# Query projection of two head groups in one matmul of 128 columns

## What is computed

```
x = x + attention0(layernorm(x), ctx, tau, delta)
x = x + ffn0(layernorm(x))
x = x + attention1(layernorm(x), ctx, tau, delta)
x = x + moe1(layernorm(x))

attention: q = split(xn @ Wq.T + bq); k, v = split(ctx @ Wk.T + bk), split(ctx @ Wv.T + bv)
           p = softmax((q k^T * tau + delta) / sqrt(8)); out = join(p v) @ Wo.T + bo
```

## Time and profile before

| | us |
|---|---|
| median of 3 runs | 214.88 (213.81 to 215.64) |
| profiled execution, device time | 216.53 |
| its span, first to last instruction | 214.7 |
| its mean granted TensorE clock | 0.935 |

### The profile page before, as it was taken

The page is one execution under the profiler, slowest core; times in us unless marked ns, Lnnn a source line. Parts: engine busy times, 40 slices in busy tenths (PEclk is TensorE's granted clock), DMA queues, the critical chain, the costliest instruction groups (busy, mean ns, idle before and its releaser), DMA issues.

```text
span 214.7 us, 3672 instructions
## 1 busy us (share of the span) xinstructions
PE 177.7 (83%) x1157; PEld 144.8 (67%) x1157; DVE 133.5 (62%) x385; ACT 90.5 (42%) x178; POOL 62.3 (29%) x68
## 2 busy tenths in 40 slices
PE   7658999999798987689978989983499749999960
PEld 2323797898684955376873769872388749999950
DVE  1899876596585359868351788455247356677750
ACT  2333146542554132531334244531354637777720
POOL 8690024000674020020006000025002734555461
PEclk9969699999999999999997999999558999999996
...
GB/s 188 277 361 406 210 2 3 0 0 3 2 93 344 112 0 0 0 5 0 0 0 3 0 0 0 3 0 99 226 48 17 89 270 28 26 5 9 20 23 2
DMA packets 11983, 15.43 MB, mean 72 GB/s; under 512 B 1713, under 2 KB 8898, under 8 KB 11965
## 3 DMA queue, kind: packets, MB, share of 16 engines
...
q10 hardware_dynamic: 432, 0.47, 0.6%
...
## 4 chain that ended last, share of the span: by engine, by line
PE 54%; DVE 22%; issue 7%; ACT 5%; DMA 4%; another core or an unknown queue 2%; POOL 2%; DVEq 1%; ACTq 0%; POOLq 0%
PE acc L911 10%; PE scores L1012 7%; PE acc L1023 6%; PE shared L850 5%; PE scores L892 4%; PE shared L968 3%; PE shared L954 3%; DVE MR L658 3%; PE shared L867 3%; DVE QG L649 2%; PE shared L941 2%; DMA X<-in_x 2%; DVE XN L604 2%; PE shared L822 2%
## 5 line engine op out<-in xcount | busy, mean ns | idle before, releaser
L911 PE MATMUL acc<-VP,P 123*128 123x128 f32 (+1 forms) x320 | 41.8, 276 | 0.9 <-ACT P L535 0.9
L911 PEld LDWEIGHTS acc<-VP,P 123*128 123x128 f32 (+1 forms) x320 | 39.8, 191 | 3.5 <-ACT P L535 2.0
L535 ACT ACTIVATE P<-scores 123x512 f32<-123x512 f32 (+1 forms) x40 | 23.1, 595 | 30.8 <-PE scores L892 24.4
L461 POOL TENSOR_TENSOR X<-X,ROWS 128x512 f32<-128x512 f32 x6 | 8.1, 1352 | 76.5 <-DVE XN L604 76.4
L1012 PE MATMUL scores<-XST,HT 128*128 128x128 f32 x176 | 26.4, 298 | 4.5 <-ACT XST L565 3.5
L658 DVE TENSOR_REDUCE MR<-shared 128x4 f32<-128x308 f32 x64 | 27.3, 472 | 2.5 <-PE shared L867 2.2
L1012 PEld LDWEIGHTS scores<-XST,HT 128*128 128x128 f32 x176 | 23.7, 210 | 6.2 <-ACT XST L565 4.7
L475 POOL DMA_INDIRECT out<-XS,token x22 | 21.4, 974 | 19.6 <-DVE XS L790 16.8
L1023 PE MATMUL acc<-W,HT 128*128 x176 | 23.2, 276 | 0.2 <-DVE XS L790 0.2
L850 PE MATMUL shared<-XNT,ATT 128*96 128x512 f32 x32 | 19.0, 710 | 4.9 <-DVE VP L644 3.1
L867 PE MATMUL shared<-KG,QG 98*128 98x308 f32 x64 | 21.0, 375 | 2.1 <-DVE QG L649 1.4
...
(10 more groups left out here) (118 smaller groups left out, 255.1 us busy)
## 6 DMA issues: line engine op xcount, KB each, us to landing
...
```

Source lines behind the costliest of these rows:

```text
L535: act.activation(P[0:w, n % NP], scores[n % 2][0:w, :], ACT.Exp).then_inc(probs_ready, 1)
L911: ins = pe.matmul(acc[qt // 2][:, c:c + VW], P[0:w, n % NP, 128 * qt:128 * qt + 128], VP[0:w, l, b, j, half], start=(t == 0 and qt % 2 == ...
```

## The change

The `q` step is now made for a pair of groups, so there are 8 instead of 16. Its matmul has 128 weight columns: 64 for each group, its 32 rows of Wq twice. ACT makes two copies from it, one for each group: 64 rows of the bank (0 to 63 or 64 to 127) to partitions 0 to 63 of `QG`. VectorE makes two subtractions: rows 0 to 31 or 64 to 95 of the bank less partitions 0 to 31 of `QG`, to partitions 64 to 95. Semaphores count groups as before; the bank is free once both groups are subtracted. In the table the pair takes the place of its even group, and the entries of the odd groups are gone. For layer 0, batch 0 the four entries become two at the front. For the three others the second pair stands where the third group stood, except layer 1, batch 1, where both pairs stand at the front. The weight array loses 128 columns (64 KB) for each layer, and its query biases are repeated over 128 partitions.

```diff
--- before.py
+++ after.py
@@ -67,7 +67,7 @@
 RS8 = 1.0 / float(np.sqrt(np.float32(DK)))
 
 
-A_K, A_Q, A_V, A_O = 0, G * QR, 2 * G * QR, 2 * G * QR + D
+A_K, A_Q, A_V, A_O = 0, G * QR, G * QR + 2 * D, G * QR + 3 * D
 A_BK = A_O + D
 A_BQ = A_BK + G
 A_BV = A_BQ + G
@@ -104,24 +104,23 @@
-        ln/0/0 xn/0/0 delta vp/0/0/0 kp/0 xt/0/0 km/0/0 q/0/0/0:3 max/0/0/0 q/0/0/3 vp/0/0/1 max/0/0/1:5 vp/0/0/2
...
-        sc/0/0/4 max/0/0/15 vp/0/1/4 q/0/1/0 pv/0/0/3 mt/0/0/1 q/0/1/1 vp/1/0/0 pv/0/0/4 sc/0/0/5 q/0/1/2 sc/0/0/6
-        pv/0/0/5 max/0/1/0:3 pv/0/0/6 sc/0/0/7 max/0/1/3:5 q/0/1/3 max/0/1/5:7 sc/0/0/8:10 pv/0/0/7 max/0/1/7:9
...
-        max/1/0/0:2 vp/1/1/2 max/1/0/2:5 wo/0/1 max/1/0/5 ln/1/1 max/1/0/6:8 q/1/0/2 vp/1/1/3 mt/1/0/0 q/1/0/3
-        sc/1/0/0 max/1/0/8 xn/1/1 max/1/0/9:11 sc/1/0/1 vp/1/1/4 pv/1/0/0 xt/1/1 gate/1 max/1/0/11 sc/1/0/2:4 pv/1/0/1
...
-        mt/1/1/0 q/1/1/3 ot/1/0 max/1/1/10:12 sc/1/1/0 max/1/1/12:14 sc/1/1/1 pv/1/1/0 max/1/1/14:16 wo/1/0 sc/1/1/2
...
+        ln/0/0 xn/0/0 delta vp/0/0/0 kp/0 xt/0/0 km/0/0 q/0/0/0:2 max/0/0/0 vp/0/0/1 max/0/0/1:5 vp/0/0/2 max/0/0/5:8
...
+        max/0/0/15 vp/0/1/4 q/0/1/0 pv/0/0/3 mt/0/0/1 vp/1/0/0 pv/0/0/4 sc/0/0/5 q/0/1/1 sc/0/0/6 pv/0/0/5 max/0/1/0:3
+        pv/0/0/6 sc/0/0/7 max/0/1/3:7 sc/0/0/8:10 pv/0/0/7 max/0/1/7:9 pv/0/0/8 max/0/1/9 mt/0/1/0 max/0/1/10 pv/0/0/9
...
+        xn/2/0 km/1/0 on/0/1 vp/1/1/1 xt/2/0 q/1/0/0 ot/0/1 max/1/0/0:2 vp/1/1/2 max/1/0/2:5 wo/0/1 max/1/0/5 ln/1/1
+        max/1/0/6:8 q/1/0/1 vp/1/1/3 mt/1/0/0 sc/1/0/0 max/1/0/8 xn/1/1 max/1/0/9:11 sc/1/0/1 vp/1/1/4 pv/1/0/0 xt/1/1
...
+        pv/1/0/5 xt/2/1 sc/1/0/8 q/1/1/0:2 max/1/1/0:2 pv/1/0/6 max/1/1/2:5 pv/1/0/7 sc/1/0/9 max/1/1/5 pv/1/0/8
+        max/1/1/6:9 km/1/1 pv/1/0/9 on/1/0 max/1/1/9 mt/1/1/0 ot/1/0 max/1/1/10:12 sc/1/1/0 max/1/1/12:14 sc/1/1/1
...
     """
     steps = []
     for entry in table.split():
@@ -351,7 +350,7 @@
             if kind == "kp":
                 return k_biased, G * key[1] + 2 * (key[2] + 1)
             if kind == "q":
-                return ql_ready, nth[key] + 1
+                return ql_ready, 2 * (nth[key] + 1)
             if kind == "mt":
                 return [(m_act, nth[key] + 1), (m_dve, nth[key] + 1)]
             if kind == "gate":
@@ -516,11 +515,13 @@
                     for b in range(B):
                         act.activation(Kt[:, :, b], Kf[:, :, b], ACT.Identity, scale=tau8[0:QR, b:b + 1]).then_inc(k_scaled, 1)
                 elif kind == "q":
-                    _, l, b, g = s
+                    _, l, b, pair = s
 
                     read(act, s)
-                    act.activation(QG[0:QR, b, g], bank(s)[0:QR, :], ACT.Identity,
-                                   bias=ATT[l][0:QR, A_BQ + g:A_BQ + g + 1]).then_inc(qh_ready, 1)
+                    for odd in (0, 1):
+                        g, r = 2 * pair + odd, slice(64 * odd, 64 * odd + 64)
+                        act.activation(QG[0:64, b, g], bank(s)[r, :], ACT.Identity,
+                                       bias=ATT[l][r, A_BQ + g:A_BQ + g + 1]).then_inc(qh_ready, 1)
                 elif kind == "mt":
                     _, l, b, half = s
                     read(act, s)
@@ -643,11 +644,14 @@
                     m = CON[0:w, C_VM + HALF * j:C_VM + HALF * (j + 1)].unsqueeze(1).unsqueeze(3).to_broadcast([w, 2, HALF, DK])
                     dve.tensor_tensor(o, v, m, ALU.mult).then_inc(v_ready, 1)
                 elif kind == "q":
-                    _, l, b, g = s
-
-                    dve.wait_ge(qh_ready, nth[s] + 1)
-                    dve.scalar_tensor_tensor(QG[64:96, b, g], bank(s)[64:96, :], ATT[l][64:96, A_BQ + g:A_BQ + g + 1],
-                                             QG[64:96, b, g].bitcast(F32), ALU.add, ALU.subtract).then_inc(ql_ready, 1)
+                    _, l, b, pair = s
+
+                    for odd in (0, 1):
+                        g = 2 * pair + odd
+                        dve.wait_ge(qh_ready, 2 * nth[s] + odd + 1)
+                        dve.scalar_tensor_tensor(QG[64:96, b, g], bank(s)[64 * odd:64 * odd + 32, :],
+                                                 ATT[l][0:32, A_BQ + g:A_BQ + g + 1],
+                                                 QG[0:32, b, g].bitcast(F32), ALU.add, ALU.subtract).then_inc(ql_ready, 1)
                 elif kind == "max":
                     _, l, b, i = s
                     n = (2 * l + b) * NQ * G + i
@@ -843,18 +847,18 @@
                     pe.matmul(bank(s)[0:w, 0:D], CTX[:, b, k0:k0 + w], ATT[l][:, A_V:A_V + D],
                               start=True, stop=True).then_inc(full[use[s][0]], 1)
                 elif kind == "q":
-                    _, l, b, g = s
+                    _, l, b, pair = s
                     pe.wait_ge(in_att[l], 16)
                     pe.wait_ge(xnt_ready, nth["xt", 2 * l, b] + 1)
                     hold(s)
-                    pe.matmul(bank(s)[0:QR, :], ATT[l][:, A_Q + QR * g:A_Q + QR * (g + 1)], XNT[:, b], start=True,
+                    pe.matmul(bank(s)[:, :], ATT[l][:, A_Q + D * pair:A_Q + D * (pair + 1)], XNT[:, b], start=True,
                               stop=True).then_inc(full[use[s][0]], 1)
                 elif kind == "max":
                     _, l, b, i = s
                     n = nth[s]
                     g, qt = divmod(i, NQ)
                     if qt == 0:
-                        pe.wait_ge(ql_ready, nth["q", l, b, g] + 1)
+                        pe.wait_ge(ql_ready, 2 * nth["q", l, b, g // 2] + g % 2 + 1)
 
                         if (l, b) == (0, 0):
                             pe.wait_ge(kg_dve, min(g, 1) + 1)
@@ -1068,9 +1072,12 @@
         for g in range(G):
             for i in range(3):
                 rows_ = slice(32 * g, 32 * g + 32)
-                for c, cb, n in ((A_K, A_BK, "k"), (A_Q, A_BQ, "q")):
-                    out[:, c + QR * g + 32 * i:c + QR * g + 32 * (i + 1)] = a[p + "W" + n][rows_].T
-                    out[32 * i:32 * (i + 1), cb + g] = a[p + "b" + n][rows_]
+                out[:, A_K + QR * g + 32 * i:A_K + QR * g + 32 * (i + 1)] = a[p + "Wk"][rows_].T
+                out[32 * i:32 * (i + 1), A_BK + g] = a[p + "bk"][rows_]
+            for i in range(2):
+                out[:, A_Q + 64 * g + 32 * i:A_Q + 64 * g + 32 * (i + 1)] = a[p + "Wq"][rows_].T
+            for i in range(4):
+                out[32 * i:32 * (i + 1), A_BQ + g] = a[p + "bq"][rows_]
         out[:, A_V:A_V + D] = a[p + "Wv"].T
         out[:, A_O:A_O + D] = a[p + "Wo"].T
         out[:, A_BV] = a[p + "bv"]
```

More of the change, by code:

```diff
@@ L112, in schedule @@
-        pv/0/0/8 max/0/1/9 mt/0/1/0 max/0/1/10 pv/0/0/9 on/0/0 max/0/1/11 sc/0/1/0:2 max/0/1/12:14 vp/1/0/1 sc/0/1/2
-        ot/0/0 pv/0/1/0 wo/0/0 ln/1/0 pv/0/1/1 xn/1/0 max/0/1/14:16 pv/0/1/2 sc/0/1/3 pv/0/1/3 xt/1/0 vp/1/0/2
-        sc/0/1/4 mt/0/1/1 vp/1/0/3 sc/0/1/5 gate/0 pv/0/1/4 vp/1/0/4 sc/0/1/6 pv/0/1/5 sc/0/1/7:9 ut/0 kp/1 hid/0/0:4
-        sc/0/1/9 out/0 vp/1/1/0 pv/0/1/6:9 ln/2/0 pv/0/1/9 xn/2/0 km/1/0 on/0/1 vp/1/1/1 xt/2/0 q/1/0/0:2 ot/0/1
-        max/1/0/0:2 vp/1/1/2 max/1/0/2:5 wo/0/1 max/1/0/5 ln/1/1 max/1/0/6:8 q/1/0/2 vp/1/1/3 mt/1/0/0 q/1/0/3
@@ L117, in schedule @@
-        sc/1/0/0 max/1/0/8 xn/1/1 max/1/0/9:11 sc/1/0/1 vp/1/1/4 pv/1/0/0 xt/1/1 gate/1 max/1/0/11 sc/1/0/2:4 pv/1/0/1
-        max/1/0/12 ut/1 max/1/0/13 pv/1/0/2 hid/1/0 max/1/0/14 hid/1/1 max/1/0/15 hid/1/2 mt/1/0/1 hid/1/3 pv/1/0/3
-        sc/1/0/4 out/1 sc/1/0/5 pv/1/0/4 sc/1/0/6:8 ln/2/1 xn/2/1 pv/1/0/5 xt/2/1 sc/1/0/8 q/1/1/0:3 max/1/1/0:2
-        pv/1/0/6 max/1/1/2:5 pv/1/0/7 sc/1/0/9 max/1/1/5 pv/1/0/8 max/1/1/6:9 km/1/1 pv/1/0/9 on/1/0 max/1/1/9
-        mt/1/1/0 q/1/1/3 ot/1/0 max/1/1/10:12 sc/1/1/0 max/1/1/12:14 sc/1/1/1 pv/1/1/0 max/1/1/14:16 wo/1/0 sc/1/1/2
@@ new lines, in schedule @@
+        sc/0/0/2 pv/0/0/0:2 vp/0/1/3 max/0/0/11:13 pv/0/0/2 xt/0/1 max/0/0/13 sc/0/0/3 km/0/1 max/0/0/14 sc/0/0/4
+        max/0/0/15 vp/0/1/4 q/0/1/0 pv/0/0/3 mt/0/0/1 vp/1/0/0 pv/0/0/4 sc/0/0/5 q/0/1/1 sc/0/0/6 pv/0/0/5 max/0/1/0:3
+        pv/0/0/6 sc/0/0/7 max/0/1/3:7 sc/0/0/8:10 pv/0/0/7 max/0/1/7:9 pv/0/0/8 max/0/1/9 mt/0/1/0 max/0/1/10 pv/0/0/9
+        on/0/0 max/0/1/11 sc/0/1/0:2 max/0/1/12:14 vp/1/0/1 sc/0/1/2 ot/0/0 pv/0/1/0 wo/0/0 ln/1/0 pv/0/1/1 xn/1/0
+        max/0/1/14:16 pv/0/1/2 sc/0/1/3 pv/0/1/3 xt/1/0 vp/1/0/2 sc/0/1/4 mt/0/1/1 vp/1/0/3 sc/0/1/5 gate/0 pv/0/1/4
@@ new lines, in schedule @@
+        vp/1/0/4 sc/0/1/6 pv/0/1/5 sc/0/1/7:9 ut/0 kp/1 hid/0/0:4 sc/0/1/9 out/0 vp/1/1/0 pv/0/1/6:9 ln/2/0 pv/0/1/9
+        xn/2/0 km/1/0 on/0/1 vp/1/1/1 xt/2/0 q/1/0/0 ot/0/1 max/1/0/0:2 vp/1/1/2 max/1/0/2:5 wo/0/1 max/1/0/5 ln/1/1
+        max/1/0/6:8 q/1/0/1 vp/1/1/3 mt/1/0/0 sc/1/0/0 max/1/0/8 xn/1/1 max/1/0/9:11 sc/1/0/1 vp/1/1/4 pv/1/0/0 xt/1/1
+        gate/1 max/1/0/11 sc/1/0/2:4 pv/1/0/1 max/1/0/12 ut/1 max/1/0/13 pv/1/0/2 hid/1/0 max/1/0/14 hid/1/1
+        max/1/0/15 hid/1/2 mt/1/0/1 hid/1/3 pv/1/0/3 sc/1/0/4 out/1 sc/1/0/5 pv/1/0/4 sc/1/0/6:8 ln/2/1 xn/2/1
```

9 lines of the change are left out of this document (4 added, 5 removed).

## The result

The changed kernel takes 220.57 us (median of 4 runs, 218.75 to 221.04), the kernel before on the same chip 215.26 us. The ratio is 1.027, 95% interval 1.022 to 1.032. The forecast was 213.9 us, so both sign and size were wrong.

A forecast was written before the change was run, and what follows sets the result against it. TensorE, busy 83% of the span, was taken to count only where others wait for it; VectorE bounds the start. Terms -0.1 - 0.3 + 0.5 - 1.05 = -0.95 took 214.88 to 213.9 us, range 211.9 to 216.3.

The forecast's parts named there:

- Price of a pair: Each query pair: matmul as for one group, 0.87 us at full clock; copies 683 ns, subtractions 747 ns, numbers unchanged.
- A: Start, layer 0, batch 0 (13 to 20 us): VectorE bounds, four subtractions in a row save an idle piece, -0.1 us.
- B: Layer 0, batch 1 (33 to 48 us): late exponential +0.6, fourth group's matmul gone -0.87, net -0.3 us.
- Both waits: Layer 0, batch 1: score matmul waits for the maxima copy until 36.85; exponential ends at 40.2, probability matmul 0.6 us late.
- C: Layer 1, batch 0 (79 to 92 us): second subtraction delays the maxima copy, normalisation 0.5 us late, +0.5 us.
- D: Layer 1, batch 1 (114 to 131 us): two half-clock matmuls instead of three, maxima and a later exponential sooner, -1.05 us.
- the recorded -0.7 and -1.0: Layer 1, batch 1: maxima begin 0.7 us sooner, at 119.8; a later exponential begins 1.0 us sooner, near 127.4.
- "-0.3" at full clock: Layer 1, batch 1 without half clock: 0.4 us lost ahead of the maxima, 0.7 saved later, -0.3 us.
- the clock: Rival: fewer matmul columns make TensorE's clock fall once or twice more, sum +0.65 or +2.25 us; chance 0.1.
- the same three slices: Assumed length of each further half-clock stretch, three 1 us slices; where TensorE bounds, it costs half, 1.6 us.
- The 0.35 for the forecast: Chance given to the likeliest case, 213.9 us, with its own range 213.2 to 214.8 us.
- the third place: Query projections of layer 1, batch 0 (79 to 92 us), where the forecast was +0.5 us.

The follow-up runs named there:

- x7: Kernel before, plus unused short bf16 matmuls where TensorE waits, at the start (20) and in layer 1, batch 0 (15); ratio 1.013.
- y1: The changed kernel run again unaltered, six runs on a third chip, against the kernel before; ratio 1.018.
- y3: Changed kernel plus 20 unused short matmuls in TensorE's waits at the start only; ratio to the kernel before 1.014.
- x8: Changed kernel with its own table, plus unused short matmuls in TensorE's waits at the start and in layer 1, batch 0; ratio to the kernel before 1.018.
- y2: Changed kernel plus 15 unused short matmuls in TensorE's waits in layer 1, batch 0 only; ratio to the kernel before 1.020.
- x5: Changed kernel's pairs in the table of before, with an unused 96-column matmul where each odd group's step stood; ratio to the kernel before 1.015.
- x2: Kernel before with odd groups' query matmuls in one bf16 pass instead of two fp32 passes, nothing moved; ratio 0.994.

## Why the prediction was wrong

**The sum was about right for a clock that does not change, in part by luck.** By its own steps:

- *Price of a pair*: right. 683 and 745 ns; the cross-partition forms cost nothing.
- *A, -0.1*: from the first XN to the second 22.17 us against 22.62, -0.45, with 3.4 us more at half clock; where the 0.35 beyond the forecast comes from was not looked into. The four subtractions do stand in a row, as the changed kernel's chain shows (start us, us, what), where before there were three, a maximum and the fourth:

```profile
16.34 0.74 DVE QG L652
...
17.11 0.71 DVE QG L652
...
17.89 0.74 DVE QG L652
...
18.67 0.76 DVE QG L652
```

  The rest of the -0.82 at the start is a first XN that came 0.37 us sooner, as in all later profiles (6.7 to 7.1 us), x7's with the weight arrays of before among them. It is not the change's.
- *B, -0.3*: +0.08. Both waits came where they were predicted. Timeline of the changed kernel:

```profile
33.72 1.52 DVE L652 SCALAR_TENSOR_TENSOR QG<-shared,ATT,QG 32x512 fp32r<-32x512 f32 x2 [1.16 <-ACT QG L523]
...
35.27 0.69 DVE L668 CAST QG<-shared 6x512 fp32r<-6x512 f32 x1
...
36.06 0.47 PE L896 MATMUL scores<-QG,KG 102*123 102x512 f32 x1 [0.65 <-issue]
...
38.85 0.60 ACT L536 ACTIVATE P<-scores 123x512 f32<-123x512 f32 x1
...
39.50 1.16 PE L915 MATMUL acc<-VP,P 123*128 123x128 f32 x8 [0.55 <-ACT P L536]
```

  The trace of the changed kernel runs 0.82 us ahead here. So the copy that was at 35.31 is now at 35.27 + 0.82 = 36.09 (36.06 was worked out), TensorE waits 0.65 us for it, and the exponential ends at 39.45 + 0.82 = 40.27 (40.2). What is missing of the gain lies behind that; which wait took it was not tested.
- *C, +0.5*: right in mechanism, +0.35 in the profile of y1, where the clock held through it (XNT 76.64 to XN 90.40, 13.76 us against 13.41). Its timeline has both subtractions in one, then the copy, and TensorE waiting 2.39 us for it, in the order worked out from the earlier trace rows:

```profile
86.70 1.52 DVE L652 SCALAR_TENSOR_TENSOR QG<-shared,ATT,QG 32x512 fp32r<-32x512 f32 x2 [0.43 <-ACT QG L523]
...
88.58 0.69 DVE L668 CAST QG<-shared 6x512 fp32r<-6x512 f32 x1
...
89.37 0.46 PE L896 MATMUL scores<-QG,KG 102*123 102x512 f32 x1 [2.39 <-issue]
...
90.40 1.11 DVE L605 TENSOR_SCALAR XN<-X,mean_var,rstd 128x128 f32<-128x128 f32 x4
```

- *D, -1.05*: -0.94, with the clock at half for as long as before and at the same point (0.90 over both stretches, from 6.3 us behind the X sum). The maxima follow two subtractions behind the second matmul, where before they followed one behind the third:

```profile
122.74 1.52 DVE L652 SCALAR_TENSOR_TENSOR QG<-shared,ATT,QG 32x512 fp32r<-32x512 f32 x2 [0.18 <-ACT QG L523]
...
124.29 2.02 DVE L662 TENSOR_REDUCE MR<-shared 128x4 f32<-128x308 f32 x5
```

  It holds only for a fall at that point. With the same table y3, whose clock fell there too, takes 16.98 us. x8 and y2, whose 3.4 us at half clock begin 10.7 us behind the X sum, take 17.81 and 17.78: nothing is gained. How the recorded -0.7 and -1.0 add up to -1.05 the prediction does not say. Its "-0.3" at full clock is not tested. At full clock y1 takes 16.41 and x5 16.77 us, but no profile has the table of before at full clock in this place (x7: 17.65, with 3.4 us at half).

Sum: -0.45 + 0.08 + 0.35 - 0.94 = -1.0 us, where the prediction had -0.95. That they agree so closely is luck: A came 0.35 lower and B 0.38 higher than forecast, and D depends on where the clock falls.

**The step that failed is the clock.** The prediction had the mechanism as a rival, with 0.1, and priced it at "the same three slices", 1.6 us, once or twice. Measured in the profile pair: 6.8 us low from 82 to 89 and 10.2 from 92 to 103 us, 17 us instead of 3 to 7. It costs 3.86 us behind place C and 0.79 + 0.60 - 0.35 = 1.04 us in it, 4.9 together. That is 0.29 us for each us at half clock, where the prediction took 0.5, so its length was sized too short and its price too high. With the -1.0 of the four places, the earlier XN (-0.37) and 0.54 behind D that makes the +4.1 us of the spans. The 0.54 are +0.93 between the two ROW sums (16.86 and 17.79 us) and -0.39 behind; in the changed kernel the clock fell 2.3 us ahead of the second of these sums, before 1.0 us behind it. Three misreadings led to it. I took the falls in the trace of before to be at 23 and 115 us and looked for new ones there. But that trace has three more: at 13 to 16 us, at 211 to the end, and the longest at 149 to 163:

```profile
149.00:163.00 14.00, 9.36 (x44) 8.23 (x45) 6.48 (x31) 6.75 (x14) 0.00 (x0) 0.51 0.38 115
```

The place where the change thinned the work most, at full clock and with VectorE as the bound (C), I had priced by its queues alone. In B I had written that the 0.87 us taken out "buys nothing; TensorE just waits", and in neither did I ask what TensorE's use became: in C 2.92 us of 4.1 went to 2.14 of 4.2. And I took the clock of one trace for that of the kernel, where the three times of before (213.81 to 215.64) already held its spread. The 0.35 for the forecast stood on a clock that I had no reason to hold fixed.

Shown are four things. The time follows the low time (y1, x2). Less load brings more falls with the order of before (x2), and the order alone brings none with the load of before (x5). The fall that cost most is made in the third place (y3 against y2, and the profiles of all kernels). And the second halves' order costs 0 to 3 us where nothing is gained (x5) and seems to take back most of what the smaller load could give (x2 against y1). Open is what decides between fall and no fall in one program, and why the first set of runs (low times 37 to 51 in all four) fell more often than y1's six.
